# One resident load of the second feed-forward weight in place of eight half loads

## What is computed

```
h   = gelu(xn @ ternary(W1).T + b1)      # [2048, 1024] -> [2048, 4096]
out = h @ ternary(W2).T + b2             # [2048, 4096] -> [2048, 1024]
x   = x + L1_attn(xn) + out
```

## Time and profile before

| what | us |
|---|---|
| median of 2 timed runs | 8685.93 |
| the two runs | 8628.15 and 8743.71 |
| the profiled execution, its own time | 8088.69 |
| its span on the slowest core (core 0) | 8086.9 |
| spans of the eight cores | 8056.2 to 8086.9 |

### The profile page before, as it was taken

How to read it: one execution, slowest core, us unless ns; L and a number is a source line. 1 busy time by engine, 2 the same in 40 slices (tenths; PEclk the granted TensorE clock), 3 DMA queues, 4 the chain that set the end, 5 groups by cost and what they waited for, 6 DMA issues and landing times.

```text
span 8086.9 us, 72415 instructions; the slowest of 8 cores (8056.2 to 8086.9 us)
## 1 busy us (share of the span) xinstructions
PE 6020.8 (74%) x25392; PEld 2490.3 (31%) x25392; DVE 2371.6 (29%) x4977; ACT 1738.3 (21%) x2768; POOL 152.4 (2%) x177
## 2 busy tenths in 40 slices
PE   3354899999997886887886777946746667676687
PEld 1111344443443333333333333422211122222233
DVE  4633222222222222222223222246343422323000
ACT  1000111111111111111111111110043556474121
POOL 0000000000000000000000000000000000000000
PEclk9555899999998998998997888968867677777898
DMA  1000323323413113113113211111112020201423
GB/s 51 5 0 1 60 50 63 61 37 75 84 42 65 37 37 73 37 32 58 29 31 74 48 39 39 21 44 24 22 36 32 1 32 1 32 1 16 131 65 81
DMA packets 165181, 336.80 MB, mean 42 GB/s; under 512 B 13171, under 2 KB 54940, under 8 KB 162404
## 3 DMA queue, kind: packets, MB, share of 16 engines
q0 software_dynamic: 107888, 221.31, 16.0%
q1 hardware_dynamic: 56948, 110.85, 4.4%
HBM read 445.96 MB, written 46.14 MB: 61 GB/s over the span
## 4 chain that ended last, share of the span: by engine, by line
PE 64%; DMA 11%; DVE 10%; ACT 6%; issue 6%; DVEq 3%; SPq 0%; POOL 0%; ACTq 0%; POOLq 0%
PE pA L706 22%; PE pB L722 11%; PE pC L722 11%; ACT expT L1091 4%; PE pA L1210 3%; DMA wbuf<-L_W 2%; DMA denM<-den_stg 2%; DMA w1t_sc<-buf 2%; PE pB L1224 2%; PE pC L1224 1%; PE pD L620 1%; PE pC L1113 1%; PE pA L1082 1%; DVE zT L1128 1%; DVE den_stg L1125 1%
## 5 line engine op out<-in xcount | busy, mean ns | idle before, releaser
L706 PE MATMUL pA<-xnT,W1q 128*128 128x512 bf16 x8192 | 1820.1, 384 | 0.0
L711 ACT ACTIVATE h<-pA,b1c 128x512 bf16<-128x512 f32 x1024 | 703.5, 687 | 3720.5 <-PE pA L706 3720.5
L706 PEld LDWEIGHTS pA<-xnT,W1q 128*128 128x128 bf16 x8192 | 808.7, 99 | 985.5 <-issue 46.0
L736 DVE SCALAR_TENSOR_TENSOR acc<-pB,G,acc 128x512 f32<-128x512 f32 x512 | 383.3, 751 | 2243.3 <-PE pB L722 1644.3
L722 PE MATMUL pB<-W2q,h 128*128 128x512 bf16 x4096 | 940.2, 380 | 127.5 <-ACT h L711 120.0
L722 PE MATMUL pC<-W2q,h 128*128 128x512 bf16 x4096 | 937.6, 379 | 0.0
L722 PEld LDWEIGHTS pB<-W2q,h 128*128 128x128 bf16 x4096 | 384.2, 98 | 642.9 <-issue 214.7
L1091 ACT ACTIVATE expT<-pA,shcol 128x512 bf16<-128x512 f32 (+1 forms) x704 | 462.0, 735 | 415.1 <-PE pA L1082 358.7
L736 DVE SCALAR_TENSOR_TENSOR acc<-pC,G,acc 128x512 f32<-128x512 f32 x512 | 384.0, 751 | 536.3 <-PE pC L722 349.3
L722 PEld LDWEIGHTS pC<-W2q,h 128*128 128x128 bf16 x4096 | 390.2, 98 | 482.2 <-issue 29.0
L1098 DVE TENSOR_TENSOR expT<-expT,s_masks 128x512 bf16<-128x512 bf16 (+1 forms) x640 | 270.0, 425 | 810.1 <-ACT expT L1091 781.7
(11 more groups left out here) (253 smaller groups left out, 3616.6 us busy)
## 6 DMA issues: line engine op xcount, KB each, us to landing
W1q<-L_W POOLq DMA_DIRECT2D x32, 2048.0 KB, 19.3
W2q<-L_W POOLq DMA_DIRECT2D x32, 2048.0 KB, 32.6
wbuf<-L_W SPq DMA_DIRECT2D x32, 1024.0 KB, 13.0
w2tb<-w2t_sc POOLq DMA_DIRECT2D x8, 4096.0 KB, 16.9
wbuf<-L_W SPq DMA_DIRECT2D x32, 512.0 KB, 10.7
wbuf<-L_W SPq DMA_DIRECT2D x64, 256.0 KB, 4.9
WOb<-L_WO POOLq DMA_DIRECT2D x8, 2048.0 KB, 15.6
o<-stg POOLq DMA_DIRECT2D x64, 256.0 KB, 4.0
```

Source lines behind the costliest of these rows:

```text
L706: t_p1 = mm.mark(TE.raw.matmul(PS[bk], lhsT=W1q[:, s, a, ft * 128:(ft + 1) * 128], rhs=xnT[:, a, tq * 512:(tq + 1) * 512], start=(a == 0), ...
L711: bank_free[bk] = sc.mark(SE.raw.activation(h1[:, ft, :], PS[bk], ACT.Relu, bias=b1c0[:, e, qq * 8 + ft:qq * 8 + ft + 1]))
L736: bank_free[bk] = vv.mark(VE.raw.scalar_tensor_tensor(out=aslc, in0=PS[bk], scalar=G[:, tq * 4 + ts_, e:e + 1], in1=aslc, op0=OP.mult, op1 ...
```

## The change

`w2tb` becomes [128, 32, 1024], which is the same number of bytes, and holds the scratch tensor as it lies in DRAM. It is loaded once ahead of the loop, behind `w1tb` on the same queue. The loads in the loop go, and with them the waits that guarded the slots. The matmuls read `w2tb[:, fc, dch*512:(dch+1)*512]`, again 512 neighbouring columns. Everything else stays.

```diff
-                    w2tb = sbl(st, "w2tb", (128, 2, 32, 512), BF16)
+                    w2tb = sbl(st, "w2tb", (128, 32, 1024), BF16)
...
                     t_w1t = dma(GE, ffws[0], w1tb[:], w1t_sc, deps=(tk["tern"],))
-                    t_w2use = [None, None]
+                    t_w2t = dma(GE, ffws[1], w2tb[:], w2t_sc,
+                                deps=(tk["tern"],))
                     t_stg_used = [None, None]
                     t_huse = mm.tok()
                     for tq in range(max(1, NCH)):
                         for dch in range(2):
-                            ws = dch
-                            t_w2t = dma(GE, ffws[1 + dch], w2tb[:, ws, :, :],
-                                        w2t_sc[:, :, dch * 512:(dch + 1) * 512],
-                                        deps=(t_w2use[ws], tk["tern"]))
...
-                                        rhs=w2tb[:, ws, fc, :],
+                                        rhs=w2tb[:, fc, dch * 512:(dch + 1) * 512],
...
-                            t_w2use[ws] = mm.tok()
```

## The result

| | before | changed |
|---|---|---|
| median of all runs, us | 8392.96 (17 runs) | 8139.27 (18 runs) |
| lowest and highest | 8080.61 to 8743.71 | 7997.25 to 8663.9 |
| profiled execution, own time | 8088.69 | 8023.1 |
| spans of its cores | 8056.2 to 8086.9 | 7962.2 to 8021.5 |

The ratio is 0.9895, with a 95% interval from 0.9861 to 0.9929: 85 us of 8089, or 56 to 112 us by the interval. It is taken without the runs, about half of either kernel's, in which some cores stood part of the time at a granted TensorE clock near 0.81 and which are 1 to 10% longer, and these are also why the two medians lie 254 us apart. The saving came out as forecast (85 us, 1.0%). The absolute time did not: 8601 us was forecast with a range from 8450 to 8700, and 8139 us came.

What follows compares the result with a forecast made beforehand. TensorE was taken to bound the last stage; 75.9 us of waits for w2tb plus 8.7 us of slow restarts made 84.6, taken as 85 us off the 8685.9 us median: 8601 us, range 8450 to 8700.

Steps and rivals of the forecast that it cites:

- What bounds the stage, and why four waits and not eight: Last stage: TensorE bounds it, 129 us idle; only half 1's load is late, behind half 0's output DMAs on POOL.
- The four waits, 75.9 us: Last stage, border between the halves of each chunk: TensorE's four waits for w2tb go, 75.9 us saved.
- The slow restarts, 8.7 us: Groups behind the four waits: without a gap the clock does not fall, another 8.7 us saved.
- Nothing takes the wait's place: Border between the halves: no other wait appears, and the group pitch of 7.33 us runs through.
- The new load: Head of the last stage: w2tb lands behind w1tb, 36 us ahead of its first reader, costing zero.
- The sum, 85 us: Last stage: waits and restarts give 84.6 us, the chunk pitch 85.0 us; taken as 85 us, -1.0%.
- The base it was taken from: Whole kernel: the 85 us subtracted from the timed runs' median, 8685.9 us, not the profiled 8088.7, giving 8601 us.
- case C: Whole kernel: faster by more than 2%, through other conditions only, a repeat reading about 8004 to 8450 us; chance 0.10.
- Rival B: Last stage: denser TensorE work brings a lower clock; at 0.76 net 60 us slower, 8746 us; chance 0.03.

Runs made afterwards that it cites:

- e1: Against the kernel before: half 0 of w2tb still reloaded in every chunk, half 1 loaded once at the head of the stage; ratio 0.9892.
- e2: Against the kernel before: half 0 of w2tb loaded once, half 1 reloaded in every chunk; 8153 to 8902 us, all six runs with some cores at lower clock.
- e3: Against the kernel before: all eight w2tb loads kept, but both of a chunk issued at its head; ratio 0.9891.
- e6: Changed kernel plus a reload of a quarter of half 1 (1 MB) at the old late place in every chunk; 8060.73 us (one timed run).
- e5: Changed kernel with the two weight loads on POOL's queue swapped, w2tb ahead of w1tb; 8020.67 us (one run).
- e9: Changed kernel once more, unaltered, on one chip with the kernel before; 8002.21 to 8803.45 us in 10 runs, ratio 0.9913.

## Why the prediction was right or wrong

- **What bounds the stage, and why four waits and not eight: right.** e1, e2 and e3 show it apart: the covered half costs 0.1 us per chunk, the late half everything, and the early issue of the same bytes recovers all of it.
- **The four waits, 75.9 us: right.** None is left. **The slow restarts, 8.7 us: right for core 0**, and e6 puts the same price (9.1 us for four) on gaps half as long. Core 0 was one of the cheap ones: the eight cores lost 8.4 to 10.9 us in the same four groups.
- **Nothing takes the wait's place: right.** 7.33 us through the border, 114.98 us between up-projections against 115.0.
- **The new load: right.** It landed 36 us ahead of its reader and cost TensorE 1.2 us at the head in the mean, where zero was taken; e5 confirmed the reading of the landing times as one load after the other, and the other orders cost 10.5 and 21.1 us.
- **The sum, 85 us: right.** Ratio 0.9895 against a forecast of 0.990. The interval alone would allow 56 to 112 us; what carries the size is the stage in the traces, 82 us shorter in the mean of the cores.
- **The base it was taken from: wrong, and this step failed.** I wrote "nothing in it shows where these lose their time" and then "I subtract the same 85 us from the median", a median of two runs, 8628 and 8744. By what came after, both were long ones (their clocks are not on record). Fifteen more runs of the same kernel brought its median to 8393 and its lowest to 8081 us. Their level is set by the time that cores stand near 0.81, which e9's rows and the two lines show; the runs of either kernel spread over 660 us because of it, eight times the effect. The profiled 8089 us was the clearest sign of the undisturbed level, and I treated it as the odd one out: 8139 us lies in the stretch from 8004 to 8450 that case C left to other conditions, case C had 0.10, and the lower end went only a quarter of the way down to it. The numbers at hand already allowed 8004 to 8660 us (85 us below the profiled and below the longest execution), and that range would have held 8139. The forecast of the ratio needed none of this.
- **Rival B: not what happened, but what I held against it was too strong.** One execution with 1000 us at a clock of 1.00 does not say that dense matmuls leave the clock alone. In e1 and e9 they did not. The price in the rival was about right: a stage at 0.81 takes 92 us more (e1, core 1), so the gain would have been used up. The "some 550 us" of work without rest in it should have been the 512 us forecast for the stage. The rule of the Trainium skill (TensorE: Matmul & The Clock Gate, Seeing it yourself), a limit at 13/16 = 0.8125 of the clock for a whole die, agrees with the 0.81 of e1's row and 0.82 of e9's. It does not agree in two points. With eight dense cores the limit need not set in: the changed kernel's profile stands at 1.00. And where it does, it does not hold the whole die: cores 2 and 3 have 1.00 beside cores 0 and 1 with 0.82 in e9. The lower clock struck both kernels; no run shows that the change brings it on. What makes a pair of cores fall in one execution and not in the next stays open.

## What to carry to other kernels

A double-buffered load is only as early as its place in the program of the queue that issues it: behind an instruction that waits for the consumer of the present buffer, the second buffer is of no use. Look for waits that are fewer than the loads, and ask what stands ahead of the late ones; here moving the issue was worth as much as dropping the traffic. And where timed runs and the profile differ by more than the effect sought, forecast the ratio, and take the whole distance into the range of the absolute time.

## What the runs showed of the hardware that I had not expected

- A late load has a high fixed price: 4 MB land in 16.2 to 17.8 us and 1 MB in 7.0 to 9.0 us, both in rows of 1 KB, with eight cores loading. The line through 16.6 and 8.7 us has 2.6 us per MB and 6 us at zero, an estimate from two sizes. Loading a quarter of the bytes late still costs half of the wait.
- The restart of the clock costs 2.2 us per gap at 19 us of idling, and 2.3 us at 10.6 us (core 0, in the mean; single gaps on all cores 1.8 to 3.0 us and, where no core was near 0.81, 1.5 to 2.9 us).
- A third level of TensorE's clock, 0.81 to 0.82 of full speed, can hold through a stage on two neighbouring cores (0 and 1, 2 and 3, 4 and 5, 6 and 7) while the other two of the die have 1.00, and can be gone in a later stage of the same execution (e9, cores 0 and 1).
